# Combining the experts' results inside the next norm, and a norm whose GpSimd part is the power alone

## The reference

```
def layer_norm(x, w, b):
    mu = jnp.mean(x, axis=-1, keepdims=True)
    var = jnp.mean(jnp.square(x - mu), axis=-1, keepdims=True)
    return (x - mu) * jax.lax.rsqrt(var + LN_EPS) * w + b
...
def rmsnorm(x, w):
    return x * jax.lax.rsqrt(jnp.mean(x * x, axis=-1, keepdims=True) + EPS) * w
...
logits = jnp.einsum('bsh,he->bse', x, Wr)
probs = jax.nn.softmax(logits, axis=-1)
topk_w, topk_idx = jax.lax.top_k(probs, TOP_K)
topk_w = topk_w / jnp.sum(topk_w, axis=-1, keepdims=True)
...
gate = jax.nn.silu(jnp.einsum('th,ehi->tei', xf, Wg))
hidden = gate * jnp.einsum('th,ehi->tei', xf, Wu)
out = jnp.einsum('tei,eih,te->th', hidden, Wd, cw)
```

## Time and profile before

| | |
|---|---|
| median of 3 runs | 2513.24 us (2512.84 to 2515.31) |
| span of the profiled execution, first to last instruction | 2512.3 us |
| what lies around the span, against the median | 0.9 us |
| PE busy, share of the span | 2097.1 us, 83% |
| DVE | 1811.2 us, 72% |
| ACT | 1619.7 us, 64% |
| POOL | 516.8 us, 21% |

### The profile page before, as it was taken

The page is one execution under the profiler, slowest core; times in us unless marked ns, Lnnn a source line. Parts: engine busy times, 40 slices in busy tenths (PEclk is TensorE's granted clock), DMA queues, the critical chain, the costliest instruction groups (busy, mean ns, idle before and its releaser), DMA issues. The chain is left out here.

```text
span 2512.3 us, 44054 instructions
## 1 busy us (share of the span) xinstructions
PE 2097.1 (83%) x15464; PEld 900.5 (36%) x15464; DVE 1811.2 (72%) x4863; ACT 1619.7 (64%) x2370; POOL 516.8 (21%) x797
## 2 busy tenths in 40 slices
PE   6486488778377799999999987848999999999696
PEld 2365255556155222222222236731222222222375
DVE  7733695442595899999999925378999999996443
ACT  3043355333254489999999963434999999999443
POOL 6175221156112000000000005720000000000065
PEclk9598599789599699999999988965999999999798
DMA  2312560311570601011011021115011011010212
GB/s 67 95 47 72 84 121 5 95 37 50 101 136 3 155 16 30 16 30 30 16 30 30 2 74 34 54 36 151 16 30 30 16 30 31 16 30 2 74 47 87
DMA packets 94697, 127.17 MB, mean 51 GB/s; under 512 B 20906, under 2 KB 72592, under 8 KB 94480
## 3 DMA queue, kind: packets, MB, share of 16 engines
q1 hardware_dynamic: 82832, 102.99, 19.0%
q0 software_dynamic: 11648, 21.36, 2.9%
HBM read 79.88 MB, written 42.40 MB: 49 GB/s over the span
## 5 line engine op out<-in xcount | busy, mean ns | idle before, releaser
L1358 DVE TENSOR_REDUCE pair_mx<-ps 128x1 f32<-128x512 f32 x1520 | 958.7, 682 | 73.0 <-PE ps L1168 71.1
L1318 ACT ACTIVATE prob<-ps 128x1024 f32<-128x1024 f32 x1024 | 986.7, 1026 | 33.9 <-PE ps L1203 19.4
L1168 PE MATMUL ps<-k_stack,q_stack 48*128 48x512 bf16 x2048 | 573.0, 403 | 28.5 <-PEq L928 9.5
L1217 PE MATMUL ps<-prob,v_head 128*32 128x512 f32 x4096 | 547.3, 606 | 1.6 <-ACT prob L1318 1.0
L1203 PE MATMUL ps<-q_stack,k_stack 51*128 51x512 bf16 x2048 | 448.2, 384 | 12.6 <-ACT prob L1318 10.4
L1168 PEld LDWEIGHTS ps<-k_stack,q_stack 48*128 48x128 bf16 x2048 | 149.4, 94 | 498.4 <-DVE pair_mx L1358 341.8
L2240 DVE TENSOR_TENSOR hid<-silu,ps 128x256 f32<-128x256 f32 (+1 forms) x190 | 87.8, 463 | 247.1 <-PE ps L2093 168.4
L1292 ACT ACTIVATE qk<-ps 128x512 f32<-128x512 f32 x264 | 157.6, 597 | 83.0 <-PE ps L1168 72.3
L1710 DVE CUSTOM_DVE_ANT_0 ps<-ps,mask 128x256 f32<-128x256 f32 (+2 forms) x512 | 179.6, 417 | 41.1 <-PE ps L1514 39.0
L1203 PEld LDWEIGHTS ps<-q_stack,k_stack 51*128 51x128 bf16 x2048 | 102.4, 93 | 296.5 <-ACT prob L1318 254.0
L2093 PE MATMUL ps<-weight_raw,block 128*128 x632 | 192.6, 428 | 0.0
(11 more groups left out here) (249 smaller groups left out, 2285.1 us busy)
## 6 DMA issues: line engine op xcount, KB each, us to landing
q_stack<-image_dram SPq DMA_DIRECT2D x88, 192.0 KB, 4.5
k_stack<-k_wide_dram SPq DMA_DIRECT2D x60, 240.0 KB, 5.6
arena<-e_rows SPq DMA_DIRECT2D x32, 256.0 KB, 4.7
k_stack<-image_dram SPq DMA_DIRECT2D x32, 192.0 KB, 4.3
image_dram<-parts SPq DMA_DIRECT2D x28, 192.0 KB, 5.3
k_wide_dram<-parts SPq DMA_DIRECT2D x2, 1800.0 KB, 17.2
image_dram<-parts SPq DMA_DIRECT2D x28, 128.0 KB, 5.0
weight_raw<-in_L_ffn_Wg_dram SPq DMA_DIRECT2D x6, 528.0 KB, 5.0
```

What stands on the lines that cost most here:

```text
L1168: nc.tensor.matmul(max_bank(n), rows_of(c.q_stack, b, g, ROWS, slice(t * P, (t + 1) * P)), rows_of(c.k_rows, b, g, ROWS, slice(k * CHUNK, ...
L1217: ins = nc.tensor.matmul(out, c.v_head[:, e % 2, kb, :], unit, start=(kb == 0), stop=(kb == TILES - 1), skip_group_check=True)
L1318: nc.scalar.activation(c.prob[:, u % P_UNITS, :], c.ps[:, 2 * (u % 2) * CHUNK:2 * (u % 2) * CHUNK + UNIT], ACT.Exp, scale=scale).then_inc( ...
L1358: ins = nc.vector.reduce_max(mx[:, w:w + 1], max_bank(n), AX.X)
```

## The change

1. **Combining moves.** `experts_stage` ends after its last block. A new class `Combine` has the waits for the scatters, the loads (SP), the scaling (ACT) and the adding (DVE); it is handed as `before` to the norm that follows (c, e, g) or to `store_stage`, which stores the result in four DMAs, each behind its chunk.
2. **Norms.** Epsilon is added by DVE ("widen"), GpSimd does only the power. The lag is one chunk everywhere. In `double_norm_stage` the power over each chunk covers only the root that the normalise needs; the other root is done once, for all 16 columns, at the end.
3. **Ranking** of chunk k stands three steps behind its statistics and no longer behind everything.
4. **Weights.** SP loads the last group of experts (three of nine, two of eight) at the start of `experts_stage`.

The core of the diff:

```diff
-            def statistics(g):
-                tiles = slice(g * TPC, (g + 1) * TPC)
+            def measure(g):
                 for t in range(g * TPC, (g + 1) * TPC):
                     ins = nc.vector.bn_stats(c.bn[:, t, :], src[:, t, :])
-                chain.link(ins)
+                ins.then_inc(measured.sem, 1)
+
+            def aggregate(g):
+                dve.wait_ge(*measured.after(g + 1))
                 for t in range(g * TPC, (g + 1) * TPC):
                     ins = nc.vector.bn_aggr(c.mv[:, t, :], c.bn[:, t, :])
+                ins.then_inc(moments_ready.sem, 1)
+
+            def widen(g):
+                tiles = slice(g * TPC, (g + 1) * TPC)
+                dve.wait_ge(*moments_ready.after(g + 1))
...
+                else:
+                    ins = nc.vector.tensor_scalar(c.rstd[:, tiles], c.mv[:, tiles, 1], eps, None, ALU.add)
+                ins.then_inc(widened.sem, 1)
...
-            lag = 2 if router is None else 1
-            for g in range(CHUNKS + lag):
+            for g in range(CHUNKS + 1):
                 if g < CHUNKS:
                     if before is not None:
                         before.vector(dve, g)
-                    statistics(g)
-                if g >= lag:
-                    normalise(g - lag)
+                    measure(g)
+                    aggregate(g)
+                    widen(g)
+                if g:
+                    normalise(g - 1)
+                if router is not None and g >= RANK_LAG:
+                    rank(chain, g - RANK_LAG)
             if router is not None:
-                rank(chain)
+                for k in range(CHUNKS + 1 - RANK_LAG, CHUNKS):
+                    rank(chain, k)
...
-                pool.wait_ge(*stats_ready.after(g + 1))
-                pool.tensor_scalar(c.rstd[:, tiles], c.mv[:, tiles, 1], eps, None, ALU.add).then_inc(rstd_ready.sem, 1)
-                pool.wait_ge(*rstd_ready.after(2 * g + 1))
-                pool.tensor_tensor(c.rstd[:, tiles], c.rstd[:, tiles], c.minus_half[:, tiles], ALU.pow)\
-                    .then_inc(rstd_ready.sem, 1)
+                pool.wait_ge(*widened.after(g + 1))
+                pool.tensor_tensor(c.rstd[:, tiles], c.rstd[:, tiles], c.minus_half[:, tiles], ALU.pow).then_inc(rstd_ready.sem, 1)
...
-                load_all_weights(c, sp, weights)
-                store_rows(c, sp, dst)
...
+                    load_group_weights(c, sp, weights, expert_groups(weights[0].shape[0])[:-1])
+                    store_rows(c, sp, dst)
...
+class Combine:
+    def sync(self, sp):
+        for b in range(SCATTERS):
+            sp.wait_ge(*self.scattered[b].after(len(range(b, self.blocks, SCATTERS)) * 16))
+        for k in range(CHUNKS):
+            for s in range(2):
...
+                sp.dma_start(c.results[:, s, k * TPC:(k + 1) * TPC, :], rows).then_inc(self.results[k].sem, 16)
...
+    def vector(self, dve, k):
+        dve.wait_ge(*self.results[k].after(32))
+        for t in range(k * TPC, (k + 1) * TPC):
+            ins = nc.vector.scalar_tensor_tensor(c.x[:, t, :], c.results[:, 0, t, :], c.total[:, t:t + 1], c.x[:, t, :],
+                                                 ALU.mult, ALU.add)
+        ins.then_inc(self.first_added.sem, 1)
+        dve.wait_ge(*self.first_added.after(k + 1))
+        dve.wait_ge(*self.scaled.after(k + 1))
+        tiles = slice(k * TPC, (k + 1) * TPC)
+        nc.vector.tensor_tensor(c.x[:, tiles, :], c.x[:, tiles, :], c.results[:, 1, tiles, :], ALU.add).then_inc(self.combined.sem, 1)
+        dve.wait_ge(*self.combined.after(k + 1))
...
         @block.sync
         def _(sp):
...
+            load_group_weights(c, sp, (gate_w, up_w, down_w), expert_groups(E)[-1:])
...
-            combine(dve, chain)
...
-            sp.dma_start(out.rearrange("b (t p) d -> p (b t) d", p=P), c.x[:]).then_inc(stored.sem, 16)
-            sp.wait_ge(*stored.after(16))
+            for k in range(CHUNKS):
+                sp.wait_ge(*before.combined.after(k + 1))
+                tiles = slice(k * TPC, (k + 1) * TPC)
+                sp.dma_start(rows[:, tiles, :], c.x[:, tiles, :]).then_inc(stored.sem, 16)
+            sp.wait_ge(*stored.after(CHUNKS * 16))
```

More of the change, by code:

```diff
@@ L500, in _ @@
                         before.vector(dve, g)
[L501 to L506, removed]
+                    measure(g)
+                    aggregate(g)
+                    widen(g)
+                if g == CHUNKS - 1:
+                    dve.wait_ge(*moments_ready.after(CHUNKS))
+                    nc.vector.tensor_scalar(c.rstds[:, 0, :], c.mv[:, :, 1], LN_EPS, None, ALU.add).then_inc(first_widened.sem, 1)
+                if g:
+                    normalise(g - 1)
+            dve.wait_ge(*first_rstd.after(1))
             nc.vector.scalar_tensor_tensor(c.kept_bias[:], c.mv[:, :, 0], -1.0, c.rstds[:, 0, :], ALU.mult, ALU.mult)\
                 .then_inc(kept_ready.sem, 1)
-            links[0] = chain.n
         @block.gpsimd
@@ L2389, in experts_stage, with store_stage @@
         s.passed(n)
-def store_stage(c, out):
+def store_stage(c, out, before):
     nc = c.nc
@@ L2516, in experts @@
             held, m = c.layer(held_by)
-            with held:
-                c.weight_raw, c.down, c.block = (m[x] for x in ("weight_raw", "down", "block"))
-                c.rows_in, c.rows_out, c.silu, c.hid, c.hidt = (m[x] for x in ("rows_in", "rows_out", "silu", "hid", "hidt"))
-                c.results = m["arena"][:].bitcast(fp32).rearrange("p (k t d) -> p k t d", k=2, d=D)
-                low, one, high = 2 * TILES * P, 2 * TILES * blocks, 4 * TILES * blocks
-                c.one_low = m["arena"][:, 0:low].rearrange("p (i n) -> p i n", n=P)
-                c.one = m["arena"][:, low:low + one].rearrange("p (i n) -> p i n", n=blocks)
-                c.one_high = m["arena"][:, low + one:low + one + high].rearrange("p (i a n) -> p i a n", a=2, n=blocks)
-                c.pick, c.both, c.spread, c.slots, c.iota_high = (m[x] for x in ("pick", "both", "spread", "slots", "iota_high"))
-                c.filled, c.n_blocks, c.ends, c.begins = (m[x] for x in ("filled", "n_blocks", "ends", "begins"))
-                c.passed, c.block_of, c.block_expert = (m[x] for x in ("passed", "block_of", "block_expert"))
-                c.place, c.place_i, c.split_i, c.split = (m[x] for x in ("place", "place_i", "split_i", "split"))
-                c.table = m["table"]
-                c.empty, c.second_pick, c.row, c.spare, c.unused = (m[x] for x in ("empty", "second_pick", "row", "spare", "unused"))
-                c.gather_ids, c.scatter_ids = m["gather_ids"], m["scatter_ids"]
-                if shared:
-                    c.shared_raw, c.shared_down = m["shared_raw"], m["shared_down"]
-                norm(router=router, weights=[i[w] for w in weights], shared=[i[w] for w in shared] if shared else None)
-                experts_stage(c, E, soft_of_probs, *(i[w] for w in weights), inner, scale=scale, shared=bool(shared), residual=c.h if shared else None)
@@ new lines, in experts @@
+            c.weight_raw, c.down, c.block = (m[x] for x in ("weight_raw", "down", "block"))
+            c.rows_in, c.rows_out, c.silu, c.hid, c.hidt = (m[x] for x in ("rows_in", "rows_out", "silu", "hid", "hidt"))
+            c.results = m["arena"][:].bitcast(fp32).rearrange("p (k t d) -> p k t d", k=2, d=D)
+            low, one, high = 2 * TILES * P, 2 * TILES * blocks, 4 * TILES * blocks
+            c.one_low = m["arena"][:, 0:low].rearrange("p (i n) -> p i n", n=P)
+            c.one = m["arena"][:, low:low + one].rearrange("p (i n) -> p i n", n=blocks)
@@ new lines, in experts @@
+            c.one_high = m["arena"][:, low + one:low + one + high].rearrange("p (i a n) -> p i a n", a=2, n=blocks)
+            c.pick, c.both, c.spread, c.slots, c.iota_high = (m[x] for x in ("pick", "both", "spread", "slots", "iota_high"))
+            c.filled, c.n_blocks, c.ends, c.begins = (m[x] for x in ("filled", "n_blocks", "ends", "begins"))
+            c.passed, c.block_of, c.block_expert = (m[x] for x in ("passed", "block_of", "block_expert"))
+            c.place, c.place_i, c.split_i, c.split = (m[x] for x in ("place", "place_i", "split_i", "split"))
@@ new lines, in experts @@
+            c.table = m["table"]
+            c.empty, c.second_pick, c.row, c.spare, c.unused = (m[x] for x in ("empty", "second_pick", "row", "spare", "unused"))
+            c.gather_ids, c.scatter_ids = m["gather_ids"], m["scatter_ids"]
+            if shared:
+                c.shared_raw, c.shared_down = m["shared_raw"], m["shared_down"]
+            norm(router=router, weights=[i[w] for w in weights], shared=[i[w] for w in shared] if shared else None)
+            experts_stage(c, E, soft_of_probs, *(i[w] for w in weights), inner, scale=scale, shared=bool(shared), residual=c.h if shared else None)
@@ L2537, in experts0 @@
+            return Combine(c, blocks, held)
         def experts0():
[L2538 removed]
```

(1 more changed line is left out.)

230 lines of the change are left out of this document (122 added, 108 removed).

## The result

The changed kernel takes 2533.78 us, median of 4 runs (2533.26 to 2537.85), against 2514.27 for the kernel before in the same runs: a ratio of 1.0078, 95% interval 1.0062 to 1.0093. It is slower by some 20 us. The forecast was 2510.2, with a range of 2506.0 to 2514.5, and slower had a chance of 0.05.

A forecast was written before the change was run, and what follows sets the result against it. PE and DVE carry the unchanged attention and expert blocks; at touched stretches, the last engine opening the barrier decides. Terms -3.0-0.9+2.6+1.3-0.9+1.6+1.3+2.4-1.4 gain 3.0: span 2509.3, plus 0.9, 2510.2 us; range 2506.0 to 2514.5.

The forecast's parts named there:

- the one on the junctions: Expert stages into e's and g's norms: norm loses 1.0, hidden 0.53 barrier passage returns some; 0.45 lost each, 0.9 together.
- c's junction: From b's experts through c's double norm to the next stage: 20.17 us against 22.76, a gain of 2.6.
- the store: Result stored in quarters at the end: only the last is exposed, 2.0, and a 0.4 passage saved; gain 2.4.
- Rival 2: Expert stage's barrier not hidden, POOL waits for its scatters: 4 x 0.53 = 2.1 paid before the loads; 2512.3, chance 0.15.
- Rival 3: GpSimd's power held up beside DVE's normalise: eight norms' tails grow 0.84, total 2516.9; chance 0.10, worse half above 2518.3, 0.05.
- Rivals 1 and 4: 16-column power: short as the eight-column one, with warm start 2506.4, chance 0.23; or four short ones long, 4.16, total 2513.9.
- the plain norms: a's two norms and c's second: widening on DVE and waiting at lag one lose 1.0 each, 3.0 together.
- the routing norms: In b and d, stores free SP earlier and DVE's last rank decides: gains of 1.6 and 1.3; f and h 0.
- h's double norm: From start of statistics to next stage, 12.36 us against 13.64, a gain of 1.3.
- the weights: Eight loads moved to the expert stage's start: hidden by DVE's dispatch before the first gathered block at 130.58, no cost.
- f's double norm: Chunks first added from PSUM, then waiting for the 16-column power: 15.26 us against 14.34, a loss of 0.9.
- The clock term: c's feed-forward starts at the lower clock because its norm's transposes come in four bursts: loss 1.4, bounds 0 to 2.4.

The follow-up runs named there:

- e5: The changed kernel, with no block of the program draining GpSimd at its end: 2512.02 us, ratio 0.999.
- e9: The changed kernel again without an edit, for a second profile: 2533.96 us, ratio 1.0079 to the kernel before.
- e7: The kernel before, with no block draining GpSimd at its end: 2517.43 us, ratio 1.0011.
- e10: The changed kernel with no block draining GpSimd, the plain norms of the kernel before, and the 16-column power cut into four: 2506.56 us, ratio 0.9965.
- e3: The kernel before, without the GpSimd drain at the end of the expert stages: 2527.5 us, ratio 1.0047.
- e6: The changed kernel with no block draining GpSimd and the plain norms of the kernel before: 2507.34 us, ratio 0.9968.
- e4: The changed kernel without the drain at the end of the expert stages, plain norms with two chunks of lag: 2521.53 us, ratio 1.0029.
- e8: The changed kernel with its drains, but SP issues the loads of results at the expert stage's end, ahead of the barrier: 2519.36 us, ratio 1.0015.
- e1: The changed kernel, without the GpSimd drain at the end of the expert stages: 2524.58 us, ratio 1.0037.

## Why the prediction was wrong

**The step that failed** is the one on the junctions: "the 0.53 passage disappears into the time in which SP waits for the scatters (POOL comes to the barrier at 235.65 ...)". POOL issued its last scatter by 235.65 and came to the barrier 6.6 us later, behind its drain. It was taken as one fact that an engine has no more instructions in the timeline and that it is at the barrier. The profile counts a drain as no busy time, so the timeline has no row for it; the source view of the block's line had it in the trace of before, 7.6 to 7.8 us four times, and the prediction does not use it. The sentence is on the junctions of e and g, and the terms of c's junction and the store rest on the same reading. At 5.4 us for each of four junctions this is 21.6: 2510.2 + 21.6 = 2531.8, for a measured 2533.78. e5, which takes the drains out and leaves all else, measured 2512.02 for 2510.2. The two leftovers, 2.0 and 1.8 us, agree, and e5 is 3.3 us (0.3 to 5.0 by its interval) below the kernel before, where the prediction had 3.0.

**Rival 2** had the place right (the expert stage's barrier waits for POOL), but not the reason, a wait for the scatters: they have landed 1.3 us after the issue, and the drain goes on to 6.6. It priced the wait at one passage of 0.53, where 5.4 was to be paid, and was argued down with the very 1.35 us that show nothing of the drain. Its chance of 0.15 stood at 2512.3, some 21 us too low. Rival 3, for which I kept the slower side, did not happen: the powers over four columns stayed at 1.01 to 1.11 us beside DVE's normalise, and the contention that the Trainium skill, "GPSIMD Engine Reference", Specifications, describes shows in none of these rows. Rivals 1 and 4 are out by the row of 2.90 us. (The prediction's low end stands as rival 1 in full, which is 2506.4 by its own sum and not 2506.0; nothing hangs on it.)

**Right by their own steps:** the plain norms (1.1 for 1.0), the routing norms, where DVE's last rank ended 0.35 us ahead of the next stage as foreseen, h's double norm (1.3), c's junction once the drain is out (20.18 for 20.17), e's and g's junctions and the store from the last scatter on (e5), and the weights: b's first gathered block comes to PE 20.8 to 20.9 us into the stage before and after, and no wait of PE for weights stands in the profile after.

*f's double norm* belongs here too, though its row in the table has the other sign. These are DVE's first addition and PE's next stage, in e9, against the earlier trace rows:

```profile
814.01 0.69 DVE L1860 TENSOR_TENSOR x<-x,ps 128x512 f32<-128x512 f32 x1 [3.19 <-PE ps L1844]
...
829.19 3.75 PE L955 MATMUL ps<-ht,proj 128*128 128x512 f32 x4 [1.71 <-PEq L484]
```

They are 15.18 us apart, for 15.26 foreseen; before, they were 14.34 apart. What shortened the row is the wait for PE ahead of the first addition, 3.19 in place of 5.72. It is not the change's doing: e7, which has the double norm of before, waits 3.27. Over the twelve profiles the whole stage takes 17.3 to 20.7 us, with either double norm.

**The clock term** of 1.4 rests on a reading that the runs do not bear out: that a run of 12 transposes makes the next stage begin at the upper level. c's feed-forward did get longer, 31.69 for 29.31, and began at 0.50, the 1.2 GHz level (its norm's transposes came in runs of 4, 4 and 8). But these two windows of its first 3.41 us are of e7, which has the norm of before with its 12 transposes in one run:

```profile
450.33:453.74 3.41, 3.30 (x4) 1.51 (x5) 2.50 (x4) 1.97 (x2) 0.00 (x0) 0.50 0.01 2
```

and of e10, with the same norm:

```profile
446.59:450.00 3.41, 3.31 (x8) 1.63 (x9) 2.50 (x4) 3.11 (x4) 0.00 (x0) 1.00 0.00 0
```

One begins at 0.50 (stage length 32.36), one at 1.00, the 2.4 GHz level (29.38), and e7 transposes in the same runs as the kernel before:

```profile
445.96 3.29 PE L422 MATMUL ps<-ident,n 128*128 128x128 f32 x12 [1.67 <-DVE n L361]
```

So the run of transposes does not decide it alone. Of the five kernels with the plain norm of before, two begin this stage at 1.00 (before and e10) and three at 0.50 (e3, e6, e7; 31.07 to 32.36 us); the seven others all begin at 0.50 (31.69 to 32.28), e4 with its one run among them. Whether the norm's form has a part in it stays open; one profile of each kernel does not tell a cause from a coincidence of 2 to 3 us. By the Trainium skill, "TensorE: Matmul & The Clock Gate", Part 1, sustained activity brings back the upper level; that agrees with e7, whose stage begins at 0.50 and ends at 1.00 with PE at work, and does not tell the two kernels apart.

## What to carry to other kernels

Before work is moved out of the shadow of a barrier, ask of each engine when it *arrives* there, not when its last busy row ends; query the source line of the block for what is no busy time. In this kernel a block whose GpSimd issued indirect DMAs owes a drain of some 6.5 us at the next place that drains. 8 us of DVE work hid it in the kernel before, and loads issued ahead of it hid the larger part in e8. Every DMA here has a semaphore of its own that is waited for, so the drain could be left out; but left out of the expert stages alone it came back in the next norm (e1, e3), and only without it in every block (e5) was its price gone.

## What the runs showed of the hardware

- GpSimd's drain at the end of an expert stage ends 6.4 to 6.6 us past the last issue of an indirect DMA, and it does not wait for the transfers: begun 20 us after the last one (e1), it still took 6.56 more than a drain without them (10.565 for 4.004 us), and 6.42 in a block where GpSimd had nothing else to do (e1). All four expert stages issue 78 to 80 indirect DMAs, so whether the price depends on their number is not shown.
- GpSimd's power costs 1.03, 1.67 and 2.90 us for 4, 8 and 16 columns. A line through them has 0.41 us fixed and 0.156 for each column.
- One program was granted a mean clock of 0.54 and of 0.67 over the same 21 us of the same stage in two executions, and the stage took 61.8 and 58.95 us: a difference of that size between two single profiles does not show what an edit does.
